# A selective scan whose states are weighted by C: in TensorE's moving operand in place of ScalarE's scale

## The reference

```
deltaA  = exp(einsum('bld,dn->bldn', delta, a))
deltaBu = einsum('bld,bln,bld->bldn', delta, b, u)
step:     h = dA_t * h + dBu_t
          y = einsum('bdn,bn->bd', h, c_t)
y = y + x_b * D_param
y = y * silu(res)
return y @ out_proj_w.T + out_proj_b
```

## Time and profile before

| | |
|---|---|
| median of 3 runs | 658.33 us (658.2 to 660.86) |
| profiled execution | 657.73 us |
| its span | 656.0 us |
| around the span | 1.73 us |
| granted clock of TensorE, mean | 0.996 |
| scan loop, first to last scan's start | 194.7 to 357.3 us |

### The profile page before, as it was taken

One profiled execution on the slowest core, in us unless ns is written; L12 is line 12 of the kernel. 1 busy time (PEld: TensorE's weight loads), 2 busy tenths in 40 slices (PEclk: granted clock), 3 DMA queues, 4 the chain that ended last, 5 costly groups with the idle time before them and its releaser, 6 DMA issues. The chain is left out here.

```text
span 656.0 us, 11718 instructions
## 1 busy us (share of the span) xinstructions
PE 602.4 (92%) x4436; PEld 460.0 (70%) x4436; DVE 465.2 (71%) x798; ACT 368.7 (56%) x700; POOL 235.1 (36%) x190
## 2 busy tenths in 40 slices
PE   7999999999998778878788999999999899999997
PEld 6645555464366667767677888887777768889897
DVE  2753433347767999999999517788978878886554
ACT  2311111136889999999999333344656465555343
POOL 2000000000089999999898200035651022231000
PEclk8999999999999999999999999999999999999999
DMA  9999999984903232233220000000100022210001
GB/s 335 407 415 416 416 418 414 420 324 159 258 12 107 106 104 97 97 98 126 99 97 1 1 1 17 1 0 19 36 2 2 1 65 85 61 49 1 32 1 33
DMA packets 32831, 87.52 MB, mean 133 GB/s; under 512 B 8092, under 2 KB 20840, under 8 KB 30600
## 3 DMA queue, kind: packets, MB, share of 16 engines
q1 hardware_dynamic: 32088, 86.18, 35.7%
q10 hardware_dynamic: 688, 0.59, 0.3%
HBM read 84.53 MB, written 1.11 MB: 131 GB/s over the span
## 5 line engine op out<-in xcount | busy, mean ns | idle before, releaser
L847 POOL TENSOR_TENSOR dbu<-du,bs 128x1024 f32<-128x1024 f32 x64 | 149.8, 2365 | 7.0 <-DVE w_in L1095 4.6
L976 ACT ACTIVATE weighed<-T,CT 128x256 f32<-128x256 f32 x222 | 94.9, 592 | 1.2 <-PE T L1174 0.9
L1095 DVE TENSOR_TENSOR_SCAN w_in<-hS,dbu 128x1024 f32<-128x1024 f32 x42 | 94.6, 2271 | 0.4 <-ACT hS L965 0.4
L965 ACT ACTIVATE hS<-delta,negA 128x504 f32<-128x504 f32 x128 | 90.7, 813 | 5.3 <-DVE xn L1095 2.5
L1188 PE MATMUL Y<-ident,weighed 128*128 128x128 f32 x512 | 66.8, 273 | 0.1
L1174 PE MATMUL T<-ident,w_in 128*128 128x128 f32 x336 | 45.9, 279 | 19.8 <-ACT weighed L976 13.8
L1188 PEld LDWEIGHTS Y<-ident,weighed 128*128 128x128 f32 x512 | 57.8, 141 | 0.9 <-DVE sres L1119 0.3
L1174 PEld LDWEIGHTS T<-ident,w_in 128*128 128x128 f32 x336 | 36.1, 140 | 30.7 <-DVE w_in L1095 27.4
L1095 DVE TENSOR_TENSOR_SCAN xn<-hS,dbu 128x1024 f32<-128x1024 f32 x22 | 50.0, 2274 | 2.3 <-ACT hS L965 2.3
L425 POOL COPY w_xp<-w_xp 128x64 f32<-128x64 f32 x3 | 0.6, 234 | 138.8 <-DMA w_out<-in_w_out 138.8
L314 PE MATMUL O<-cN,pT 123*64 123x256 f32 (+1 forms) x384 | 46.7, 385 | 3.8 <-DMA cN<-in_ctx 3.1
(11 more groups left out here) (444 smaller groups left out, 1340.7 us busy)
## 6 DMA issues: line engine op xcount, KB each, us to landing
cN<-in_ctx SPq DMA_DIRECT2D x8, 3072.0 KB, 24.3
cT<-in_ctxT SPq DMA_DIRECT2D x7, 3202.0 KB, 24.5
bs<-b_rows SPq DMA_DIRECT2D x32, 512.0 KB, 3.7
raw_w<-in_w SPq DMA_DIRECT2D x16, 256.0 KB, 3.0
cT<-in_ctxT SPq DMA_DIRECT2D x1, 2178.0 KB, 12.2
cR<-in_ctx SPq DMA_DIRECT2D x8, 256.0 KB, 23.7
w<-in_w SPq DMA_DIRECT2D x7, 256.0 KB, 7.9
vs<-vx SPq DMA_DIRECT2D x8, 136.0 KB, 2.4
```

Source lines behind the costliest of these rows:

```text
L847: e.tensor_tensor(dbu[s % NB][:, :, :], half(m.du, s // DS), row, ALU.mult).then_inc(s_bu, 1)
L965: i = e.activation(by_batch(A[s % 2][:, j * HALF:(j + 1) * HALF]), by_batch(m.delta[:, c, h * HALF:(h + 1) * HALF]), ACT.Exp, scale=m.negA ...
L976: i = e.activation(weighed[s % 2][:, q * Q:(q + 1) * Q], T[:, q * Q:(q + 1) * Q], ACT.Copy, scale=c_of(s, q))
L1095: e.tensor_tensor_scan(S[s % NS], A[s % 2][:, :], dbu[s % NB][:, :, :].rearrange("p c n -> p (c n)"), 0.0, ALU.mult, ALU.add).then_inc(s_h, 1)
```

## The change

The weights by C move from ACT and DVE into PE's second matmul. For each state and each half of the tokens, DRAM holds four 128 x 128 matrices side by side (128 rows of 512 words) that are zero off their diagonals and have C on them. A transfer from a zeroed tile clears the region; the diagonal entries are written by transfers of single words; for each two steps one load brings two states' matrices (512 KB) into one of three slots, two made of the finished `k.xT` and one of `k.xz`. PE's add is a plain f32 matmul, turned states by diagonal, in place of a transposing one against the identity. ACT copies two halves of 512 columns without a scale, and DVE no longer weighs. C's small transposes and `CT` go. On SP, the clearing and the diagonal writes stand between the transfers of B. Four further clearings and the second half's diagonals are issued in the loop, at groups 6 to 9 and at group 12.

Two small edits do not concern the scan: a semaphore of the cross-attention is merged into another (`s_q0` into `s_qr`), and the zeroing of `wfq` counts on the common semaphore of constants in place of one of its own. C's turn no longer stands in `pe_steps`, so `bv` on PE waits for the third raw gate itself.

```diff
+def clear_diagonals(e, m, h, a=0, n=DS):
+
+    e.dma_start(m.c_dram[h, a:a + n, 0:P * HALF].rearrange("n (p q) -> p n q", p=P),
+                m.blank.unsqueeze(1).to_broadcast([P, n, HALF])).then_inc(m.s_cd, 16)
+
+
+def write_diagonals(e, m, h):
+
+    for b in range(HALF // P):
+        diagonal = m.c_dram[h, :, b * P:b * P + P * (HALF + 1)].rearrange("n (t x) -> n t x", x=HALF + 1)[:, :, 0]
+        e.dma_start(diagonal, m.rows[C_AT:C_AT + DS, h * HALF + b * P:h * HALF + (b + 1) * P],
+                    allow_slow_non_contiguous=True).then_inc(m.s_cd, 16)
+
+
+def load_diagonals(e, m, g):
+
+    h = UNITS[2 * g // DS][0]
+    n = 2 * g % DS
+    e.dma_start(m.cd[g % SLOTS][:, :, :], m.c_dram[h, n:n + 2, 0:P * HALF].rearrange("n (p q) -> p n q", p=P)
+                ).then_inc(m.s_cl[g % SLOTS], 16)
...
             loads(e)
+            e.wait_ge(k.s_const, k.n_const + 1)
+            clear_diagonals(e, m, 0)
...
-            for g in range(SLOTS, STEPS // 2):
-                e.wait_ge(s_bu, 2 * (g - SLOTS) + 2)
-                load_states(e, m, g)
+                    e.wait_ge(m.s_cd, 16)
+                    write_diagonals(e, m, 0)
+            e.wait_ge(m.s_cd, 16 * 5)
+            e.wait_ge(s_fp, pe_at["in", 15])
+            for g in range(SLOTS):
+                if g == SLOTS - 1:
+                    e.wait_ge(s_fp, pe_at["b", 0])
+                load_diagonals(e, m, g)
+            for g in range(SLOTS, STEPS // 2 + 1):
+                if g < STEPS // 2:
+                    e.wait_ge(s_bu, 2 * (g - SLOTS) + 2)
+                    load_states(e, m, g)
+                if g in range(6, 10):
+                    clear_diagonals(e, m, 1, 4 * (g - 6), 4)
+                if g == 12:
+                    e.wait_ge(m.s_cd, 16 * 9)
+                    write_diagonals(e, m, 1)
+                if g == DS + 1:
+                    e.wait_ge(m.s_cd, 16 * 13)
+                if g > SLOTS:
+                    e.wait_ge(s_y, 4 * (g - 1 - SLOTS) + 4)
+                    load_diagonals(e, m, g - 1)
 
         @block.gpsimd
         def _(e):
+            e.memset(m.blank, 0.0).then_inc(k.s_const, 1)
...
-            def weigh(s, b):
+            def keep_turned(s, b):
                 e.wait_ge(s_t, 2 * s + b + 1)
                 if s >= 2:
                     e.wait_ge(s_y, 2 * (s - 2) + b + 1)
-                for q in (2 * b, 2 * b + 1):
-                    if q < 3 or not on_dve(s):
-                        i = e.activation(weighed[s % 2][:, q * Q:(q + 1) * Q], T[:, q * Q:(q + 1) * Q], ACT.Copy,
-                                         scale=c_of(s, q))
-                i.then_inc((s_e0, s_e1)[b], 1)
+                e.activation(turned[s % 2][:, b * HALF:(b + 1) * HALF], T[:, b * HALF:(b + 1) * HALF], ACT.Copy
+                             ).then_inc(s_e, 1)
...
-            def weigh(s):
-
-                e.wait_ge(s_ct, 1)
-                e.wait_ge(s_t, 2 * s + 2)
-                e.wait_ge(s_e1, s + 1)
-                if s >= 2:
-                    e.wait_ge(s_y, 2 * (s - 2) + 2)
-                e.tensor_scalar(weighed[s % 2][:, 3 * Q:4 * Q], T[:, 3 * Q:4 * Q], c_of(s, 3), None, ALU.mult
-                                ).then_inc(s_q, 1)
...
                 if b == 0:
                     e.wait_ge(s_h, s + 1)
-                    e.wait_ge(s_e0, s)
                     if s == 0:
                         e.wait_ge(s_ct, 1)
                         e.wait_ge(s_vo, 2)
-                else:
-                    e.wait_ge(s_e1, s)
-                    e.wait_ge(s_q, dve_before(s))
+                if s:
+                    e.wait_ge(s_e, 2 * s - 1 + b)
                 for q in (2 * b, 2 * b + 1):
                     for j in range(2):
                         i = e.transpose(T[:, q * Q + j * P:q * Q + (j + 1) * P],
...
-                e.wait_ge((s_e0, s_e1)[b], s + 1)
-                if b and on_dve(s):
-                    e.wait_ge(s_q, dve_before(s + 1))
+                e.wait_ge(s_e, 2 * s + b + 1)
+                if b == 0:
+                    e.wait_ge(m.s_cl[s // 2 % SLOTS], 16 * (s // 2 // SLOTS + 1))
                 for j in range(2):
                     if u and n == 0 and b == 0:
                         e.wait_ge(s_yg, 2 * (u - 1) + j + 1)
                     for q in (2 * b, 2 * b + 1):
                         i = e.matmul(Y[:, j * HALF + q * P:j * HALF + (q + 1) * P],
-                                     weighed[s % 2][:, q * Q + j * P:q * Q + (j + 1) * P], k.ident[:, :],
-                                     start=u > 0 and n == 0 and q == 0, stop=True, is_transpose=True, skip_group_check=True)
+                                     turned[s % 2][:, q * Q + j * P:q * Q + (j + 1) * P],
+                                     m.cd[s // 2 % SLOTS][:, s % 2, q * P:(q + 1) * P],
+                                     start=u > 0 and n == 0 and q == 0, stop=True, skip_group_check=True)
...
-            e.wait_ge(s_rg, 3)
-            for t in range(TILES):
-                i = e.transpose(T[:, t * 2 * DS:(t + 1) * 2 * DS], m.rows[32:64, t * P:(t + 1) * P], k.ident[32:64, 32:64])
-            i.then_inc(s_fp, 1)
...
+            m.c_dram = k.c_dram
+            m.cd = [k.xT[:, i, :].rearrange("p (n t) -> p n t", n=2) for i in range(KD)] + [k.xz]
+            m.blank = k.gated[:, 0, :]
+            m.s_cd = sem("n_cd")
+            m.s_cl = [sem(f"n_cl{i}") for i in range(SLOTS)]
```

More of the change, by code:

```diff
@@ L154, in cross_attention @@
         s_qr = sem("a_qr")
-        s_q0 = sem("a_q0")
         s_qa = sem("a_query_act")
@@ L578, in key_bias @@
                 e.tensor_tensor(xs, xs, X[:, 0:D].unsqueeze(1).to_broadcast([P, n, D]), ALU.mult).then_inc(s_qr, 1)
-                e.wait_ge(s_qr, 2 * f + 2)
+                e.wait_ge(s_qr, 3 * f + 2)
                 e.reduce_sum(qraw[:, at], xs, AX.X).then_inc(s_qr, 1)
-                e.wait_ge(s_qr, 2 * f + 3)
-                e.tensor_scalar(qbk[:, at], qraw[:, at], qconst, scale, ALU.add, ALU.mult).then_inc(s_q0, 1)
+                e.wait_ge(s_qr, 3 * f + 3)
+                e.tensor_scalar(qbk[:, at], qraw[:, at], qconst, scale, ALU.add, ALU.mult).then_inc(s_qr, 1)
             def evacuate(i, g):
@@ L595, in maximum @@
                 e.wait_ge(s_m1, i * 2 + 1)
-                e.wait_ge(s_q0, 1 if i == 0 else 2 if i < TILES - 1 else 3)
+                e.wait_ge(s_qr, 4 if i == 0 else 7 if i < TILES - 1 else 10)
                 e.tensor_scalar(full_max[:, :], mx[:, :], scale, qbk[:, i:i + 1], ALU.mult, ALU.add
@@ L710, in mamba @@
         dbu = [sb(f"dbu{i}", [P, 2, HALF]) for i in range(NB)]
-        weighed = [sb(f"weighed{i}", [P, 4 * Q]) for i in range(2)]
-        CT = sb("CT", [P, TILES, 2 * DS])
+        turned = [sb(f"turned{i}", [P, 4 * Q]) for i in range(2)]
         S = [k.xn[:, 4:8, :].rearrange("p t d -> p (t d)")] + [k.w_in[:, i, :] for i in range(2)]
@@ L717, in mamba @@
         T = ps("T", [P, 2 * HALF])
-        acc4 = [weighed[r // 2][:, r % 2 * HALF:(r % 2 + 1) * HALF].rearrange("p (b l) -> p b l", l=L) for r in range(4)]
+        acc4 = [turned[r // 2][:, r % 2 * HALF:(r % 2 + 1) * HALF].rearrange("p (b l) -> p b l", l=L) for r in range(4)]
         expA = sb("expA", [P, CH * DS])
@@ L721, in mamba @@
         spare = T[:, TILES * 2 * DS:HALF]
-        qT = weighed[0][:, 0:HALF]
+        qT = turned[0][:, 0:HALF]
         kTb = k.xz[:, :, :].rearrange("p c n -> p (c n)")[:, 0:KD * (D + 1)].rearrange("p (c n) -> p c n", c=KD)
         qk, qk_at = Y.rearrange("p (j n) -> p j n", j=KD), HALF // 2 + 8
-        vT, bvT = weighed[1][:, 0:HALF], weighed[1][:, HALF:HALF + KD]
+        vT, bvT = turned[1][:, 0:HALF], turned[1][:, HALF:HALF + KD]
         xq = [a[:, 0:HALF] for a in A]
@@ L749, in mamba @@
         s_t = sem("n_t")
-        s_e0 = sem("n_e0")
-        s_e1 = sem("n_e1")
-        s_q = sem("n_q")
+        s_e = sem("n_e")
         s_y = sem("n_y")
@@ L761, in mamba @@
         pe_steps = ([("in", n) for n in range(2, 8)] + [("xj", 0), ("in", 8), ("dt", 0), ("in", 9), ("in", 10), ("in", 11),
-                    ("xj", 1), ("in", 12), ("dt", 1), ("in", 13), ("in", 14), ("in", 15), ("wT", 0), ("wT", 1), ("CT", 0),
+                    ("xj", 1), ("in", 12), ("dt", 1), ("in", 13), ("in", 14), ("in", 15), ("wT", 0), ("wT", 1),
                     ("vo", 0), ("bv", 0), ("A", 0), ("b", 0), ("vo", 1)])
@@ L781, in half @@
             return a[:, 2 * cp:2 * cp + 2, h * HALF:(h + 1) * HALF]
[L783 to L791, removed]
         @block.sync
@@ L1008, in _ @@
                     e.preload_act_table_set("silu_and_others")
-                for b in (1, 0) if on_dve(s) else (0, 1):
-                    weigh(s, b)
+                for b in range(2):
+                    keep_turned(s, b)
                 if s == STEPS - 2:
@@ L1086, in _ @@
             e.wait_ge(s_fp, pe_at["bv", 0])
-            e.tensor_copy(bvT, spare[:, 0:KD])
```

(14 more changed lines are left out.)

1 line of the change is left out of this document (removed).

## The result

The changed kernel takes 694.09 us (median of 4 runs, 693.17 to 695.65), the kernel before 658.97 us (658.20 to 660.86): a ratio of 1.0531, 95% interval 1.0499 to 1.0563. It is 35 us slower. The forecast was 680 us with a range of 668 to 716.

A forecast was written before the change was run, and what follows sets the result against it. PE was to bound the scan loop at 2.75 us a step: from 207.4 us, 179.7 us of work and waits end at 387.1, 22.6 us later than before, put at 21.7. Forecast 680 us, range 668 to 716.

The forecast's parts named there:

- (a): The forecast itself: PE bounds the loop, first diagonals a few us late; 680 us, range 670 to 692, chance 0.60.
- (b): Rival: single-word writes of C are slow; 728 us if 8,192 take 35 us, 698 at 20 us; chance 0.26.
- the first add near 207 us: Sign at the loop's start: first add at 207.4 us, 4.0 us late, its wait ended by the load of diagonals.
- the missing wait near step 22: Sign in the loop: no add waits there for diagonals, the second half's word writes being hidden.
- (d): Rival: a plain f32 add costs four times a transposing one; 110 us more, 790 us; chance 0.02.
- PE as the new bound: Scan loop: plain adds of 1.79 us for eight bring PE to 2.67 us a step, 2.75 with D shares.
- The relief of DVE: Scan loop: DVE loses 34 weighings, 19 us; if PE kept up, POOL would bound at 650 us, chance 0.05 for faster.
- The stalls at the ends of units: Between units, PE idles while DVE gates Y and scans: about 1.2 us three times, 3.5 us.
- the first half's words: Ahead of the loop: 8,192 single-word writes of C take 8.2 us, at the rate of 256-byte pieces.
- The second half's words: At group 12: 8,192 single-word writes, 8.2 us, fit within 13.7 us of hidden time and cost nothing.
- What would have been taken back: Whole span: of the 22.6 us later end a small part is regained, leaving 21.7.
- ACT's copy: Scan loop: a 512-column copy from PSUM lasts 0.58 us, reckoned as 0.6, so ACT needs 2.4 us a step.

The follow-up runs named there:

- the half-weighted one: Changed kernel with reordered transfers and spread words; only the tokens' quarters 2 and 3 weighted by diagonals, 0 and 1 by ACT's scale: 656.31 us, ratio 0.9953.
- the other order: Changed kernel with only the second attention's weights loaded ahead of the first clearing, the later stages' weights and c0T from group 18 on: 679.07 us, ratio 1.0317.

## Why the prediction was right, and where its sizes were off

**The time.** 694.09 us lies in the whole range, 668 to 716, but outside the 670 to 692 that the prediction gave to its own forecast (a). The bound was that of (a); the 14 us between 680 and 694 are slow words and what hangs on them, as in rival (b). The range held them only because it made room for (b). Of the signs named, the count and pace of the adds, PE, DVE and ACT's copies came out; the first add near 207 us and the missing wait near step 22 did not. One sum is off: the upper half of (b) and all of (d) make a chance of 0.15 above 716, not 0.12.

**PE as the new bound: right, to the hundredth.** The prediction put an add at two records of 0.112 us, a step at 2.67 us, and 179.7 us from the first add to the end of the last. The trace shows 0.112 and 2.66, and the run without diagonals has 382.6 + 0.3 - 203.8 = 179.1 us. That run also has the time that the prediction gave for diagonals in time, 676. What mattered was to look for the neighbours of a shape that the trace did not have: two records for each plain matmul, and the load's pitch where the moving side is short. Eight plain adds take 1.79 us where eight transposing ones take 0.88: twice. The factor of four for FP32 that the Trainium skill gives (TensorE: Matmul & The Clock Gate, Terms) is not what an add of this shape costs; the runs disagree with it as a price.

**The relief of DVE: right, and of no use.** With PE's cost taken back by one flag the kernel is 10.7 us faster than before, and POOL is the bound, as the prediction named it: it gave 650 us for that case, the run 648.33.

**The stalls at the ends of units: right.** In the run without diagonals the first unit ends so:

```profile
245.51 1.04 PE L1165 MATMUL T<-ident,w_in 128*128 128x128 f32 x8
...
249.25 1.09 PE L1165 MATMUL T<-ident,xn 128*128 128x128 f32 x8 [0.59 <-DVE xn L1100]
250.18 1.95 PE L1177 MATMUL Y<-ident,turned 128*128 128x128 f32 x16
```

From 245.51 to 250.18 there are 4.67 us for two turns and an add, which need 0.88 + 1.79 + 0.88 = 3.55: 1.1 us lost, where 1.2 were forecast.

**The step that was mis-sized is the first half's words.** They were put at 8.2 us by the rate of 256-byte pieces in the earlier trace rows, with bounds of 0 and 35. With the row copy behind them they were to take 10.8 us; they took 19.8, from 191.0 to 210.8: 16 us on the engines, and then 4 us until SP knew. The parts ahead of them were nearly right: the broadcasts of B went out at 184.8 where the sum had 186.7. So the first add came at 214.8 and not at 207.4, 7.4 us more. The upper bound of 35, from SP's issue time of the eight-byte load, was about twice too high; the truth lay between. The rival of slow words holds in mechanism, at a price somewhat below the lower of its two, 20 us and 698. All these prices took a word to cost the same wherever it stands in a row, and the packets show that it does not. The Trainium skill (DMA: Bandwidth & Descriptors, Specifications) asks for 512 bytes or more for full rate; 5 GB/s agrees, though no run here shows what the engine does with a word.

**The clock was not in the sum.** The hole of 11 us on PE that the prediction had as a wait of 4 us brought the clock down: 2.3 us at the first add. At step 22 the slower records make 1.7 of the 4.2 us. That a wait costs more than its length should have been a term of its own.

**The second half's words: the hiding place was too small by a little.** 13.7 us were reckoned as hidden. SP began to issue them at 260.1 us, the group's load went out at 268.5 and landed 11.4 us later, at 279.9: 20 us, where 17.4 were at hand. From 263.0 to 274.5 us the trace has 8,249 packets under 512 bytes: the words took about 11 us here, with 3 us of other transfers ahead of them. The price was 4.2 us, where the sum had none. Spread over four groups it is gone.

**What would have been taken back was not.** The prediction took 0.9 us off; the sum of the terms as measured is 21.7 + 0.9 + 7.4 + 2.3 + 4.2 = 36.5 us, less 0.6 for the pace of PE (179.1 in place of 179.7), and the span grew by 35.8.

**ACT's copy was priced too high.** Two copies of 512 columns come 1.08 - 0.59 = 0.49 us apart and not 0.6, so ACT needs 2.2 us a step and not 2.4. It did not show in the changed kernel, as PE was the bound. It did in the half-weighted one, where 2 x 0.6 + 2 x 0.36 + 0.49 = 2.41 is the step measured, against 2.52 expected.

## What to carry to other kernels

Work that moves to the engine with the most idle time is only free up to that idle time: here PE had 0.8 us a step, and eight plain f32 matmuls in place of eight transposing ones cost 0.9. A weighting can be split between two forms so that no engine is over the next one's time; that gave the only versions with all the work done that are not slower than the kernel before, and they are faster by no more than 0.5%. Here the transfers of single words did best with an early place in the queue and 2,048 words at a time; what stands behind them waits for the last of them. PE's 11 us of waiting cost 2.3 us more by the clock, while after a wait of 1.6 us the clock had stayed up.

## What the runs showed of the hardware

- Writing words of four bytes to DRAM is not of one price: 4,096 were off the engines in about 4 us, 8,192 took 16 us at a share of 1.35 and 5 GB/s. After that 4 to 6 us passed before SP could go on, with the engines at a share of 0.01 to 0.11. Within the 8,192, the pace fell from 3,543 packets in 4 us to 1,444 in the next 4.
- SP was held for 12.0 us by the issue of four such transfers, and for 11.9 in the other order, and its next issue came only then.
- After a wait of 11.3 us PE ran its next 16 records 0.23 us apart, (3.76 - 0.28) / 15 in the mean, in place of 0.112; the granted clock was 0.50 from 214.7 to 218.3 us and 1.00 again from 222 to 226.
- On ACT a plain copy of 512 columns from PSUM takes 0.49 us in a row of them, an exponential of 504 columns with a scale for each partition 0.6, a scaled copy of 256 columns 0.36.
